# Graph kernel on one core: where the 16-bit parts of Wk and Wv are made, and another order of projection pieces and field turns

## The reference, cut to what matters

```python
h = jnp.maximum(_layernorm(x), 0.0)
q = (h @ Wq + bq)        # 512 x 512 weights, in 32-bit
k = (h @ Wk + bk)
v = (h @ Wv + bv)
attn = attn.at[b_idx, loc_src, loc_dst].add(edge_attr @ We + be)
out = x + softmax(attn) @ v @ Wo + bo
...
x = x + gcn(relu(layernorm(x)), edge counts and edge weights)
```

## Time and profile before

| | |
|---|---|
| runs | 1421.78, 1423.92, 1424.75 us; median 1423.92 |
| profiled execution | 1426.35 us, its span 1425.1 us, clock 0.984 |
| PE, DVE, ACT busy over the span | 1370.5, 887.8, 568.9 us |
| build, 64 to 434 us | 370 us: PE 348.01, DVE 339.11, ACT 225.11 us busy |
| chain that ended last, over the span | PE 84%, DVE 7%, ACT 3%, DMA 3%, issue 2% |

### The profile page before, as it was taken

How to read it: one execution, slowest core, us unless ns; L and a number is a source line. 1 busy time by engine, 2 the same in 40 slices (tenths; PEclk the granted TensorE clock), 3 DMA queues, 4 the chain that set the end, 5 groups by cost and what they waited for, 6 DMA issues and landing times.

```text
span 1425.1 us, 26631 instructions
## 1 busy us (share of the span) xinstructions
PE 1370.5 (96%) x11265; PEld 845.3 (59%) x11265; DVE 887.8 (62%) x1374; ACT 568.9 (40%) x971; POOL 87.9 (6%) x86
## 2 busy tenths in 40 slices
PE   7889999979996999999999999999999999999998
PEld 6778999969995665544444444444444445444443
DVE  6999898988995887666664766542344232532322
ACT  2665666645654447611133112412243223432322
POOL 3030011101001221000000100002200000000000
PEclk9989999999997999999999999999999999999999
DMA  9643444254337661200000100012202222553201
GB/s 321 231 141 106 136 136 152 102 169 133 124 124 246 180 212 38 84 30 0 1 1 5 55 1 0 0 30 82 82 15 59 60 76 65 214 207 104 89 0 59
DMA packets 71859, 137.95 MB, mean 97 GB/s; under 512 B 11924, under 2 KB 24340, under 8 KB 70326
## 3 DMA queue, kind: packets, MB, share of 16 engines
q1 hardware_dynamic: 69070, 125.03, 26.4%
q0 software_dynamic: 1280, 5.77, 1.6%
q10 hardware_dynamic: 1384, 5.38, 1.1%
HBM read 82.83 MB, written 53.32 MB: 96 GB/s over the span
## 4 chain that ended last, share of the span: by engine, by line
PE 84%; DVE 7%; ACT 3%; DMA 3%; issue 2%; SPq 0%; POOL 0%; ACTq 0%; DVEq 0%; POOLq 0%
PE banks L2183 31%; PE banks L2117 13%; PE banks L2247 11%; PE banks L1164 7%; PE banks L1533 3%; PE banks L1129 3%; PE banks L1112 3%; PE banks L1173 2%; DVE x_sb L825 2%; PE banks L1086 1%; PE banks L2061 1%; PE banks L1503 1%; PE banks L1174 1%; PE banks L1521 1%; PE banks L1492 1%
## 5 line engine op out<-in xcount | busy, mean ns | idle before, releaser
L2183 PE MATMUL banks<-g,count 128*128 128x512 f16 x1024 | 227.6, 379 | 0.5 <-DVE tiles L2449 0.5
L2183 PE MATMUL banks<-count,g 128*128 128x512 f16 x1024 | 223.6, 379 | 0.0
L2117 PE MATMUL banks<-w_parts,h_parts 128*128 128x512 f16 x960 | 215.3, 379 | 1.7 <-DVE g L2398 1.4
L2183 PEld LDWEIGHTS banks<-count,g 128*128 128x128 f16 x1024 | 99.5, 98 | 118.1
L2183 PEld LDWEIGHTS banks<-g,count 128*128 128x128 f16 x1024 | 99.8, 98 | 113.5 <-DVE tiles L2449 1.0
L2247 PE MATMUL banks<-g,part 128*128 128x512 f16 x768 | 165.9, 379 | 0.0
L2117 PEld LDWEIGHTS banks<-w_parts,h_parts 128*128 128x128 f16 x960 | 91.1, 98 | 115.4 <-issue 11.4
L825 DVE TENSOR_TENSOR x_sb<-eb_parts,x_sb 128x4096 f16<-128x4096 f16 x64 | 146.0, 2282 | 0.0
L1164 PE MATMUL banks<-x_sb 128*128 128x128 f16 x2048 | 127.7, 222 | 8.5 <-DVE x_sb L825 8.5
L2247 PEld LDWEIGHTS banks<-g,part 128*128 128x128 f16 x768 | 75.1, 98 | 90.6
L1164 PEld LDWEIGHTS banks<-x_sb 128*128 128x128 f16 x2048 | 121.9, 99 | 11.4 <-DVE x_sb L825 10.0
(11 more groups left out here) (334 smaller groups left out, 1905.0 us busy)
## 6 DMA issues: line engine op xcount, KB each, us to landing
weight_dram<-w_new SPq DMA_DIRECT2D x62, 256.0 KB, 2.5
count<-weight_dram SPq DMA_DIRECT2D x29, 512.0 KB, 7.1
qk_dram<-stage SPq DMA_DIRECT2D x64, 128.0 KB, 2.4
tiles<-x_dram SPq DMA_DIRECT2D x32, 256.0 KB, 3.5
x_dram<-tiles SPq DMA_DIRECT2D x32, 256.0 KB, 2.8
count<-in_x SPq DMA_DIRECT2D x4, 1024.0 KB, 11.5
h<-in_x SPq DMA_DIRECT2D x16, 256.0 KB, 5.1
h_dram<-h_t SPq DMA_DIRECT2D x8, 512.0 KB, 3.0
```

Source lines behind the costliest of these rows:

```text
L2117: mm = pe.matmul(out, m.h_parts[:, slot, zh, k], m.w_parts[:, zw, k], start=n == 0 and layer != 3, stop=n == len(passes) - 1)
L2183: mm = pe.matmul(m.agg_ps[:, b], lhs, rhs, start=i == 0 and z == 0, stop=i == NT - 1 and z == 1)
```

## The change

- Wk is loaded whole into the second half of the weight slab (`m.wk_raw`), which is free until batch 4; its parts 4 to 7 are made from there and not loaded again. ACT's slab copy of batch 4 waits for them.
- Wv is not loaded whole. Its sum of squares is made from four quarters through `w_spare` in batches 6, 8, 10, 13; PE's second total and DVE's second powers are in batch 16. Parts 8, 9, 10 are loaded after the last h turns (into `w_spare` and the two places of `keep.h`), 11 after part 8 is used, and are split in batches 36 to 39 instead of 38 to 41. The load of slab 0's h for the values waits for the low part 10.
- Pieces: two of slab 0 go from the start to batch 1, the others of each slab by `PIECES_OF_BATCH`, the values from batch 41 by `VALUES_OF_BATCH`. The h turns before: batches 1, 8, 13, 18, 24, 29, 34; after: 1, 6, 12, 17, 22, 28, 33.
- The turns of the fields go between a batch's bias and its count matmuls; on ACT their copies come ahead of the count copy and the relus ahead of `copy_part`.
- At the start the first splits are in batch 1 and not 0; the first two stores are issued ahead of the x loads; batch 1's `h_low` comes after its one-hots.
- `h_first` has a place of its own in Wk's 16-bit place, so that batch 0's count copy need not wait for it.

```diff
-SLAB_BATCHES = ((0, 1), (2,), (3, 4), (5,), (6, 7)), ((0, 1), (2,), (3,), (4, 5), (6,), (7,))
+PIECES_OF_BATCH = (2, 1, 2, 1, 2, 2, 2, 1)
+VALUES_OF_BATCH = (1, 1, 2, 1, 1, 2, 2, 2)
-V_START = 42
-SPLITS = {0: (0, 1, 2), 1: (3, 4, 5), 2: (6, 7)}
-SPLITS.update({V_START - 4 + k: (2 * KT + k,) for k in range(KT)})
+V_START = 41
+HIGHS = {1: range(KT, 2 * KT), 36: (2 * KT,), 37: (2 * KT + 1, 2 * KT + 2), 39: (2 * KT + 3,)}
+LOWS = {1: range(KT), 2: (KT, KT + 1), 3: (KT + 2, KT + 3), 37: (2 * KT,), 38: (2 * KT + 1, 2 * KT + 2), 39: (2 * KT + 3,)}
+SQUARES = {6: 0, 8: 1, 10: 2, 13: 3}
+SECOND_TOTAL = 16
 def part_place(m, j):
-    return m.w_new[:, j % 3] if j < 2 * KT and j % 3 < 2 else m.w_spare[:]
+    if j < 2:
+        return m.w_new[:, j]
+    if j == KT - 1:
+        return m.w_beside[:]
+    if KT <= j < 2 * KT:
+        return m.wk_raw[:, j - KT]
+    return m.x_pair[:, j - 2 * KT - 1] if 2 * KT < j < 3 * KT - 1 else m.w_spare[:]
...
 def projections(first_round):
-    add("start", 0, (2, 3, 4, 5, 6, 7))
+    add("start", 0, (2, 3, 4, 5))
+    pieces["start"].append(("total", 0))
+    add(1, 0, (6, 7))
     for slab in range(1, SLABS):
-        for part in SLAB_BATCHES[slab % 3 == 1]:
-            add(n, slab, part)
+        c = 0
+        while c < 2 * KT:
+            amount = 2 if slab == 1 else 1 if slab == SLABS - 1 and c >= KT else PIECES_OF_BATCH[n % NBATCH]
+            take = range(c, min(c + amount, KT if slab == SLABS - 1 and c < KT else 2 * KT))
+            add(n, slab, take)
+            c = take.stop
             n += 1
...
 def clear_prep(pool, keep, s):
-    pool.wait_ge(s["w_high"], 1)
+    pool.wait_ge(s["w_high"], KT)
...
 def build_dve(...):
-            hots(n + 1, [piece[1] for piece in pieces[n] if piece[0] == "h"])
+            hots(n + 1, [piece[1] for piece in pieces[n] if piece[0] == "h" and n > 1])
         if first_round and n == 0:
-            weight_powers()
+            weight_powers(0)
             residual(0, 1)
+        if first_round and n == SECOND_TOTAL:
+            weight_powers(1)
...
         evacuate(n)
+        if first_round and n == 1:
+            h_low(2)
+            h_low(3)
         if first_round:
-            for j in SPLITS.get(n, ()):
+            for j in LOWS.get(n, ()):
                 weight_low(j)
...
 def build_act(...):   # copy_sums
+        if n // NBATCH + 1 < GTILES and n % NBATCH == 3:
+            copy_fields(n // NBATCH + 1)
         act.wait_ge(s["batch"], n + 1)
...
+        if first_round and n == 4:
+            act.wait_ge(s["w_low"], 2 * KT)
...
+    def square_quarter(k):
+        act.wait_ge(s["in_part2"], 16 * (2 + k))
+        act.activation(m.w_spare[:], m.w_spare[:], ACT.Square, accum_out=keep.w_squares[:, 2 + k:3 + k]).then_inc(s["w_squared"], 1)
...
-        for i, piece in enumerate(pieces["start"]):
+        for i, piece in enumerate(pieces["start"][:KT]):
             copy_projected(piece)
...
-            if i == 3:
-                square(2)
+        relu(2)
+        relu(3)
     for n in range(LAST):
...
+        if first_round and n == 1:
+            for j in range(KT):
+                weight_high(j)
         copy_sums(n)
+        if first_round and n in SQUARES:
+            square_quarter(SQUARES[n])
         if first_round and n >= 4:
             copy_weights(n - 4)
         if first_round:
-            for j in SPLITS.get(n, ()):
+            for j in HIGHS.get(n, ()):
                 weight_high(j)
-        if t + 1 < GTILES:
-            if i == 3:
-                copy_fields(t + 1)
-                copy_part(t + 1)
         if n + 1 < LAST:
             for piece in pieces[n + 1]:
-                if piece[0] == "h":
+                if piece[0] == "h" and n > 0:
                     relu(piece[1])
+        if t + 1 < GTILES and i == 3:
+            copy_part(t + 1)
...
 def build_pe(...):    # behind the bias matmuls of batch n
+        if t + 1 < GTILES and i == 3:
+            turn_fields(t + 1)
...
         if n >= 4:
             turn_weights(n - 4)
-        if t + 1 < GTILES and i == 3:
-            turn_fields(t + 1)
...
 def build_sp(...):
     def load_h(slab):
-        sp.wait_ge(s["proj"], 2 * KT * SLABS + 4 * max(slab - 1, 0))
+        if slab == 0:
+            sp.wait_ge(s["w_low"], 3 * KT - 1)
+        else:
+            sp.wait_ge(s["proj"], 2 * KT * SLABS + 4 * (slab - 1))
...
+    def load_quarter(k):
+        sp.wait_ge(s["w_low"], KT)
+        if k:
+            sp.wait_ge(s["w_squared"], 2 + k)
+        sp.dma_start(m.w_spare[:], io["L0_gnn_Wv"][k * P:(k + 1) * P, :]).then_inc(s["in_part2"], 16)
...
-        sp.dma_start(m.w_raw[2], weight_view(io["L0_gnn_Wv"])).then_inc(keep.prep["in_wv"], 16)
+        for piece in pieces["early"]:
+            store_piece(piece)
         load_x(2)
         load_x(3)
...
+                    else:
+                        for j in range(2 * KT, 3 * KT - 1):
+                            load_part(j)
...
                 if piece[0] == "k" and piece[2:] == (SLABS - 1, KT - 1):
-                    load_h(0)
                     load_h(1)
+                if piece[0] == "v" and piece[2:] == (5, 1):
                     # as before: the load of qk_first
...
         if first_round:
-            for j in SPLITS.get(n + 1, ()):
-                load_part(j)
+            if 2 * KT in LOWS.get(n, ()):
+                load_part(3 * KT - 1)
+            if 3 * KT - 2 in LOWS.get(n, ()):
+                load_h(0)
+            if n + 1 in SQUARES:
+                load_quarter(SQUARES[n + 1])
```

More of the change, by code:

```diff
@@ L563, in build_memory @@
     free = keep.count[:].rearrange("p s c v g -> p (s c v g)").bitcast(F32)[:, NT * D:]
-    m.w_raw = [free[:, i * KT * D:(i + 1) * KT * D].rearrange("p (k d) -> p k d", k=KT) for i in range(3)]
-    m.h_first = free[:, 3 * KT * D:3 * KT * D + KT * SCOLS].rearrange("p (k n) -> p k n", k=KT)
+    m.wq_raw = free[:, 0:KT * D].rearrange("p (k d) -> p k d", k=KT)
+    m.wk_raw, m.x_pair = m.w_slab[:, 1], keep.h
+    m.h_first = place("h_first", [P, KT, SCOLS], F32, AT_K)
+    m.w_beside = place("w_beside", [P, D], F32, AT_K + 4096)
     m.unread = hots[:, 0:KT * D].rearrange("p (k d) -> p k d", k=KT)
@@ L628, in projections @@
             pieces[n - 1] += [("h", 2 * slab + 2), ("h", 2 * slab + 3)]
[L629 to L632, removed]
-        pieces[V_START + j * V_BATCHES // (2 * NT)].append(("v", number, j // 2, j % 2))
-        number += 1
+    assert n <= V_START
+    assert not any(piece[0] == "q" for b in range(min(b for b in HIGHS if 2 * KT in HIGHS[b]) + 1, V_START) for piece in pieces[b])
+    pieces[SECOND_TOTAL].append(("total", 1))
+    j, n = 0, V_START
+    while j < 2 * NT:
+        for _ in range(min(VALUES_OF_BATCH[n % NBATCH], 2 * NT - j)):
+            pieces[n].append(("v", number, j // 2, j % 2))
+            number += 1
+            j += 1
+        n += 1
+    assert n < LAST
     return pieces
@@ L652, in use_pieces @@
                 use(piece, ("h_copied" if piece[1] < 2 else "h_low", piece[1] + 1))
+            elif piece[0] == "total":
+                use(piece, ("w_read", 2 * piece[1] + 1))
             else:
@@ L661, in work_slots @@
         use_pieces("start")
-        use("total", ("w_high", 1))
     for n in range(LAST):
@@ L665, in work_slots @@
         use_pieces(n)
-        if n >= 4:
-            use(("chunk", n - 4), chunk_mark(n - 4, first_round))
         if t + 1 < GTILES and i == 3:
@@ L670, in work_slots @@
                 use(("fields", t + 1, f), ("turned", FGROUPS * (t + 1) + f + 1))
+        if n >= 4:
+            use(("chunk", n - 4), chunk_mark(n - 4, first_round))
     for c in range(LAST - 4, LAST):
@@ L1035, in build_act @@
                 copy_turned(piece[1])
-            else:
+            elif piece[0] != "total":
                 copy_projected(piece)
+        if first_round and n == 1:
+            for j in range(KT):
+                weight_high(j)
         copy_sums(n)
+        if first_round and n in SQUARES:
+            square_quarter(SQUARES[n])
         if first_round and n >= 4:
@@ L1120, in project @@
             for k in range(KT):
-                mm = pe.matmul(out, m.w_raw[0 if kind == "q" else 1][:, k, cols], m.h_first[:, k, :], start=k == 0, stop=k == KT - 1)
+                mm = pe.matmul(out, (m.wq_raw if kind == "q" else m.wk_raw)[:, k, cols], m.h_first[:, k, :], start=k == 0, stop=k == KT - 1)
         else:
@@ L1130, in project, with total @@
         mm.then_inc(s["proj"], 1)
+    def total(piece):
+        bank, free = uses[piece]
+        second = piece[1]
+        pe.wait_ge(s[free[0]], free[1])
+        pe.wait_ge(s["w_squared"], 2 + KT * second)
+        columns = [slice(2 + k, 3 + k) for k in range(KT)] if second else [slice(0, 2)]
+        for i, c in enumerate(columns):
+            mm = pe.matmul(m.work_ps[:, bank, 0:c.stop - c.start], keep.one.to_broadcast([P, P]), keep.w_squares[:, c],
+                           start=i == 0, stop=i == len(columns) - 1)
```

(12 more changed lines are left out.)

119 lines of the change are left out of this document (66 added, 53 removed).

## The result

The changed kernel took 1426.21 us (median of 20 runs, 1424.47 to 1429.65), the kernel before, run beside it, 1423.08 (20 runs, 1420.07 to 1425.99): ratio 1.0024, 95% interval 1.0017 to 1.003. It is **slower by about 3 us**. Forecast were 5.6 us less, and the range to 1423.5 didn't hold it.

A forecast was written before the change was run, and what follows sets the result against it. TensorE and VectorE, both nearly full, bound the build, the later one setting each batch's pace. Terms -2.3 -3.9 -8.9 -3.1 -4.6 +4.5 +6.9 +5.2 +0.6 made -5.6 us: 1423.92 to 1418.3, range 1413.0 to 1423.5.

The forecast's parts named there:

- part 6: Costed at nothing: Wv's four squares on ScalarE, later loads, GpSimd's wait for four high parts, tail after batch 63.
- rival A: TensorE falls to half clock with the new waits at 15, 31, 39: 6.7 us, giving 1425.0; chance 0.11.
- part 3: Fields' turns moved between bias and count matmuls: six tiles behind batch 8 save 3.1 us, count copy not late.
- part 1: Start without Wv's whole square and load: bias copy 8 is 2.3 us earlier, three more slab pieces done save 3.9.
- 2, stall at the values: Batch 41 to 42: Wv's quarters asked for earlier, in own places; 14.73 becomes 5.81 us, 8.9 less.
- rival B: Load of the first values' h slab late at batch 41, stall returns: 8.9 us in full, 1427.2; chance 0.06.
- 4 and 5: TensorE's old waits for one-hots, 4.6 us off; new waits and second total, 4.5, 6.9, 5.2 and 0.6 on.
- 5b: Batches 12, 28: h copies behind the residual's first half; VectorE waits 4.2 us, TensorE pays 6.9 in all.
- D: Start's gain (2.3) and three pieces (3.9) lost to h pair or half clock in batches 2 to 5: 1424.5; chance 0.08.
- C: ScalarE's copies and relus overlap better, up to 5 of 11.4 us of new waits unpaid: 1413.3; chance 0.17.

The follow-up runs named there:

- after_swap: Changed kernel with tile 1's two gathers ahead of clear_prep in GpSimd's queue; 1415.97 us, ratio 0.9948 to the kernel before.
- first set: Four kernels run on one chip to find what held the gather; the kernel before beside them took 1423.15 us.
- third and fourth set: Third: four earlier kernels run again unedited; fourth: parts undone beside after_swap; each on its own chip, kernel before 1425.01 and 1424.70 us.
- after_mid_again: Repeat of the changed kernel with batch 1's second h_low half moved behind the four low weight halves; 1422.02 us, ratio 0.998.
- fields_old: after_swap with the fields' turns and copies where the kernel before has them; 1418.38 us, ratio 0.9954; repeated 1417.93, 0.9954.
- old_both: after_swap with the fields' turns at their old place and copy_part behind the copies of h; 1414.30 us, ratio 0.9929.
- after_swap_again: after_swap run once more, unedited, on another chip; 1422.67 us, ratio 0.9981.
- after_again: The changed kernel itself run once more, beside after_swap_again; 1430.79 us, ratio 1.0047.
- swap_one_place: after_swap with Wv's last four parts again loaded one after another through w_spare; 1427.06 us, ratio 1.0016; repeated 1426.85, 1.0013.
- after_pause1: Changed kernel with VectorE waiting for tile 1's gathered records behind h_low of batch 1; 1422.03 us, ratio 0.9996.

## Why the prediction was wrong

Compared from the first gather on, with after_swap of the first set, which is the changed kernel without the held gather:

| bias copy, us from the first gather | before | predicted | after | after_swap |
|---|---|---|---|---|
| 8 | 75.2 | 72.8 | 80.8 | 72.7 |
| 42 | 277.8 | 274.0 | 283.2 | 273.3 |
| 63 | 388.4 | 382.7 | 391.5 | 381.6 |

**The step that failed** is in part 6: "The new wait of the GpSimd queue for four high parts instead of one ends about 74, as the first did." The wait did end early (first gather issued at 72.40), but I priced what stands behind it at nothing, as if an issued DMA cost its engine the same under any neighbour. It took 15.41 us instead of 2.77, with 8.90 of wait on TensorE and the half clock behind it (the turns alone 1.06 longer): +8.1 us at batch 8, +9.9 at 63. The 1.8 us between the two go with two more falls of the clock (rival A below). Without the held gather the build is 6.8 us shorter at 63, forecast 5.6.

That it comes so near is in part luck of the chip. In the third and fourth set after_swap is only 2.3 and 2.4 us under before: there a second step fails, part 3, forecast at 3.1 us less and measured at 4.7 more.

**The warning was in the profile**, and my own part 1 took away the cover. Before, the gather behind this pair took 6.05 us:

```profile
94.69 6.05 POOL L688 DMA_INDIRECT gathered<-rec_dram,idx  x1 [17.46 <-PE banks L1074]
```

The other gathers of the build take 1.07 to 2.90; I had not asked why. This one began under one-hots and ended at 100.74, in the keys' short instructions, which start at 99.23 and of which most read one input in SBUF; the later ones of 2.90 end 0.9 us into the same instructions. So an input in PSUM is not the only thing that lets a gather through.

And part 1 says that the three low halves and two short waits ahead of batch 2's one-hots go away: that moved `h_low`, the one instruction that let GpSimd through, from 76.32 to 74.04, ahead of the second gather. The low halves that took its place read only SBUF.

The Trainium skill, "SBUF — State Buffer", section "Who interferes with whom", says that VectorE and GpSimd share a pair of ports, and that a VectorE instruction with two SBUF inputs contends with a GpSimd instruction that reads SBUF (the gather reads its indices from there). By that rule such an instruction holds the gather, and one with an input in PSUM doesn't: the 15.41 and 9.48 us, and the ends at 79.01 (after_mid_again) and 77.23 (before) under `h_low`, agree. The same section of the Trainium skill says of an earlier probe that `tensor_tensor` did not stall DMA, and infers that generating descriptors needs the write side, which `tensor_tensor` leaves free; for a gather the runs here show otherwise. And that a whole run of such instructions holds it, over every seam, is what the traces add. A rival made of it would have been: the wait lasts until VectorE runs dry, some 10 us, 1418.3 + 10 = 1428. I had none on GpSimd at all.

**1, start**: right by the mark; 72.7 against 72.8 once the gather is early. No run prices it alone.

**2, stall at the values**: the place and the end are right (batch 41 to 42 took 5.81 us, as forecast, against 14.73; no wait for a part of Wv). But putting Wv's quarters back through one place in the new layout costs 4.6 us, not 8.9, and it is another wait: 4.30 us for the slab of h, the path of rival B, and not 5.84 for the last quarter as before. So 8.9 for the old stall was not tested by itself; the marks of 41 and 42 are what speaks for it.

**3, turns of the fields**: mis-sized. For 3.1 us I had copied TensorE's own saving. fields_old lies at 0.9954 in two sets; after_swap at 0.9948 in the first, 0.9 us better by the ratios and within their intervals, and 4.7 us above fields_old in the third, where the move loses. "ScalarE copies them while TensorE counts, so the count copy is not late": in three of four sets it is 1.70 us late, and what follows on ScalarE (slab, weights, the relus, and TensorE's h turns) with it.

**4 and 5**: the new waits are there. TensorE's for VectorE's one-hot products in after_swap:

```profile
PE banks L1229 <- DVE x_sb L858: 13.9, 8, 3.4
DVE h_t L785 <- ACT h_t L1012: 8.5, 5, 3.9
```

VectorE waits 3.9 for h copies twice, as forecast (4.2). TensorE's waits at batches 15, 31 and 39 are 1.96, 1.96 and 2.95, forecast 2.2, 2.2 and 3.1. For 5b I had 6.9 us; undoing its order gives 4.5, and 3.6 from fields_old (0.9954) to old_both (0.9929), so the term was in place and one and a half to two times too large. Each chunk of the sum from 8 to 42 (200.6 measured, 201.2 forecast) and from 42 to 63 (108.3, 108.7) came out within 0.6 us, with errors that offset.

**Rivals.** A (half clock with the new waits) happened in the profile of the changed kernel, behind two of its three waits of batches 15, 31 and 39:

```profile
165.27 3.06 PE L1229 MATMUL banks<-x_sb 128*128 128x128 f16 x32 [1.97 <-DVE x_sb L858]
```

```profile
308.07 2.55 PE L1229 MATMUL banks<-x_sb 128*128 128x128 f16 x32 [2.94 <-DVE x_sb L858]
```

The granted clock was 0.50 from 166 to 169 and from 310 to 312, and these bias matmuls took 3.06 and 2.55 us instead of 1.96. The sign that I had set for A, a clock below 1.0 between 120 and 430, is met. From bias copy 8 to 63 after takes 1.8 us more than after_swap, where the same three waits (1.96, 1.96, 2.95) were followed by the full clock. Other traces fall at one of these places and not at the next: the wait at batch 39 was followed by 0.50 in old_both and after_swap_again, and not in after_again. Waits of 2.1 us for h that come on top with the 1.70 us were followed by it too (after_swap_again at 138.09, swap_one_place at 139.12). So A had too small a chance and too high a price: 1.8 us for two falls, where I had 3.1 for each. B (the stall back at 41) did not happen, save in one_place. D (batch 8 no earlier) is what the profile of after shows at 8, but not by the mechanism named there. C comes nearest for after_swap of the first set, whose build is 1.1 us better than the sum, but the waits that C wanted gone are there.

## What to carry to other kernels

A DMA that GpSimd issues is work that needs a gap in VectorE's stream: before a change packs VectorE tighter, list the gathers that fall in that stretch and which instruction lets them through, and issue them ahead of it, or put an instruction with an operand in PSUM beside them; some 0.9 us is all a gather needed. Ask of every price taken from one row what its neighbours were; a row two to six times longer than its kind is a rival, not noise. And compare variants beside each other on one chip: here 4 to 5 us came and went between sets.

## What the runs showed of the hardware

- An indirect DMA on GpSimd lasted 0.95 us beside an idle VectorE (after_pause1) and up to 15.41 us while VectorE ran, back to back, instructions with both inputs in SBUF (16-bit TENSOR_TENSOR and SCALAR_TENSOR_TENSOR). The hold spans many instructions: no seam between two of them was enough. One TENSOR_TENSOR of 0.67 us with an input in PSUM was, and the keys' short instructions, most with one input, were too. A held gather ended 0.8 to 0.9 us behind the start of a pause or of an instruction with an input in PSUM.
- After a wait of 8.90 us TensorE's granted clock was at the lower of its levels (1.2 GHz; 11 turns in 2.62 us instead of 1.56), and so it was after 3.42 us in after_swap (75.14: 32 bias matmuls in 3.44 us instead of 1.96). After waits of 1.96 to 2.95 us it was at the lower one in some traces and at the upper one, 2.4 GHz, in others, at the same place of the same kernel. The length of the wait alone doesn't decide it.
- With 32-bit turns directly ahead of the count products, ScalarE waited 1.70 us for the counts in three sets of runs and 0.26 in the first, with the same instructions, for a reason that stays open; the kernel before, without that order, gave medians within 1.9 us in all four.
